# A graph-attention and message-passing kernel on one core: where in a half turn VectorE finishes a tile

## The chip, the cores and the metric

One Trainium2 chip, one of its cores. The metric is the device time of one execution in microseconds (us); the kernel before was run three times. The engines are PE (TensorE, matrix products), DVE (VectorE), ACT (ScalarE), POOL (GpSimd) and SP (SyncE, which only issues DMAs here). Each has its own instruction stream, executed in order, and they wait for each other through semaphores.

## What is computed

x is 8192 x 128, adj is an 8192 x 8192 matrix of zeros and ones, symmetric, with ones on the diagonal and about 0.4% of the rest. There are two layers, each with a layer norm before it and the residual added behind it:

```python
h = relu(layernorm(x))                       # layer 0: graph attention
Wh = h @ W;  f1 = Wh @ a1;  f2 = Wh @ a2
e = leaky_relu(f1 + f2.T, 0.2)
att = softmax(where(adj > 0, e, -9e15))
x = x + relu(att @ Wh)
h = relu(layernorm(x))                       # layer 1
node = h @ W1                                # 128 -> 16
m = einsum('nk,nkf->nf', node, einsum('nc,kcf->nkf', h, W2))
x = x + relu(adj @ m + node @ b)
```

## The kernel before, in words

**Blocks, turns, half turns.** The 8192 rows are 64 tiles of 128, in 8 blocks of 8 tiles. The attention loop (`attention_loop`, L297) goes through 8 blocks `ib`; a block is 4 turns `jg`, a turn two half turns `p`: 64 half turns in all, number n = 2i + p with i = 4 ib + jg. A half turn multiplies the 1024 rows of the block with 8 tiles of 128 neighbours. These 8 are called row tiles here; they come in four pairs k = 0 to 3, each with b = 0 and 1.

**What a half turn does for its own block.** adj comes in as float32, loaded by DMAs of the SP and ACT queues (`load_quadrants`, L325; SP loads quadrants 0 and 1 of each of four parts c, ACT 2 and 3). ACT casts each loaded part in two halves h to bytes (`cast`, L613, instruction L617), DVE transposes the bytes in squares of 32 (`turn_squares`, L1030) into the mask `mt`, four transposes (semaphore `squared`) a half turn, always for the next half turn. For each row tile DVE writes a 128 x 1024 weight tile p_sb with one instruction (`weigh`, L1109, instruction L1113). There are four buffers of p_sb, r = 2(k mod 2) + b, so a weigh of pair k waits (`p_used[r]`) until PE is done with the row tile of the same b in pair k-2; for k = 2 that is pair 0 of the same half turn. PE takes a row tile with 16 matmuls (L911). The mask is also stored to DRAM (`maskT_d`) by the ACT queue, for layer 1.

**What a half turn does for a tile of the block before.** From the second block on (56 half turns; `finish` is true) each half turn also finishes one tile m of the block before: it completes the attention output, normalises the row, and makes the message. The steps, by engine:
- DVE `finish_tile` (L1079). Step 0: `att` from the sums (L1084). Step 1: divide and relu (L1089), wait for `kept`, add x into `keep` (L1094), `bn_stats` (L1097), `bn_aggr` (L1100, semaphore `mv_done`). Step 2: wait for ACT's `std`, reciprocal (L1103), `xn` (L1106, `xn_done`). In `turn` (L1117) each step stands between the two weighs of a pair: step 0 in pair 0, step 1 in pair 1, step 2 in pair 2. After the second weigh of each pair comes one `turn_squares`.
- PE `finish_turn_h` (L885) waits for `xn_done` and transposes xn (L889). It stands in `half_turn` (L891) directly behind the first row tile of pair 2. After pair 2 PE multiplies by W1 and b (L877) and by the first half of W2 (L882, two groups), after pair 3 by the second half of W2 (L882).
- ACT `finish_tile` (L671): `std` at k = 1; at k = 2 first a cast, then relu of the transpose (L669), copies (L683, L685) and 8 scalings of PE's products by `node` (L693); 8 more at k = 3. Between `std` and the relu stand two casts.
- POOL `finish_tile` (L492): `confirm` (L477) waits until the stores of the tile before have landed and raises `kept`; then `fold` (L483) adds the 16 scaled products in three shrinking additions (L487) and a last one (L490), two instructions split the message (L502, L504), and two DMAs store `msg` and `keep`. `keep` and `msg` have two buffers each, so DVE's step 1 of tile m needs the stores of tile m-2.

```python
if finish and k < 3:
    finish_tile(k, p, u, 2 * u + p, 2 * jg + p, ib - 1)      # DVE, turn, L1129
if finish and k == 2 and b_ == 0:
    finish_turn_h(m)                                        # PE, half_turn, in front of the second row tile
```

**Setup** (the first 53 us). x is normalised, projected, and the bounds of the scores are found. DVE casts the lower halves of parts 0 to 2 of the first adj load (`first_cast`, L1037) and turns them; ACT casts part 3 and, after the exponentials (L645 to L653), the upper halves of parts 0 to 3. Between these it issues its share of the loads of the next turn (`load_upper`, L605), each part as soon as its upper half is cast; SP does so for its share. In the first turn DVE's transposes for the next turn stand one behind each pair of the second half turn.

**Layer 1.** `gather` (L946) runs four passes over the stored masks and messages, converted by DVE (L1160) and ACT (L716); during the first pass the last block's 8 tiles are finished (`finish_last`, another schedule). At the very end ACT stores the last 1024 rows (`store_out`, L762) in two groups of four DMAs, each when its rows are ready.

Of the kernel before, what the change touches and what calls it, by code (L numbers as in the profile page):

```python
# [29 lines left out]
ALU = mybir.AluOpType  # L30
# [8 lines left out]
def build(nc, x, adj, W, a1, a2, W1, W2, b, out):  # L39
# [34 lines left out]
    with ctx:  # L74
# [261 lines left out]
        def load_x_pair(eng, i, quadrants):  # L336
            for c in quadrants:
                eng.dma_start(rows_of_pair(i)[c * SQ:(c + 1) * SQ, :, :],
                              x_v[group(i, c):group(i, c) + 2].rearrange("h r t f -> r h (t f)")).then_inc(x_in[i], 16)

        def load_xt(eng, pb):
            eng.wait_ge(mv_done, T * pb + 1)
            for c in range(A):
                eng.dma_start(xt[c * SQ:(c + 1) * SQ, :, :], x_v[bass.ds(group(pb, c), 1)]
                              .rearrange("g r t f -> (g r) t f")).then_inc(xt_in, 16)


        @block.sync
        def _(sp):

            sp.sem_inc(xt_in, 16 * A)
            for i in range(1, 4):
                load_x(sp, i, (0, 1))
            for i in range(4, NB, 2):
                load_x_pair(sp, i, (0, 1))
            load_x(sp, 0, (0, 1))
            for c in range(A):
                load_quadrants(sp, 0, 0, c, (0, 1))

            def turn(i, ib, jg, rows=False):  # L360
                for c in range(A):
                    if isinstance(i, int) and i == 1:
                        sp.wait_ge(adj_cast[0][c], 1)
                    sp.wait_ge(adj_cast[1][c], i)
                    load_quadrants(sp, ib, jg, c, (0, 1))
                    if rows and c == 2:
                        load_xt(sp, ib - 1)

            def turns(ib, first, rows=False):
                for jg in range(first, IT):  # L370
                    turn(ib * IT + jg, ib, jg, rows and jg == 1)

            turns(0, 1)
            sp.dma_start(wcat[:, 0:K * D].rearrange("c (k f) -> c k f", f=D),
                         W2.rearrange("k c f -> c k f")).then_inc(w2_in, 16)
            turns(1, 0)
            with sp.Fori(0, NB - 2) as before:
                turns(before + 2, 0, True)

            for c in range(A):  # L380
                sp.wait_ge(adj_cast[1][c], NB * IT)
            for p in range(2):
                sp.wait_ge(mt_stored[p], 16 * 2 * IT)

            def load_messages(s):
                o = ORDER[s]
                sp.dma_start(msgs[:, o * T:(o + 1) * T, :, :].rearrange("p n c f -> p (n c f)").bitcast(FP32),
                             msg_d[:, o * T:(o + 1) * T, :].rearrange("p n f -> p (n f)").bitcast(FP32))\
                  .then_inc(msgs_in[s], 16)

            def load_masks(ii, s):
                q = s % 4

                if isinstance(ii, int) and s >= 4:
                    sp.wait_ge(conv_dve, dve_count(True, (s - 3) * T - 1, 1))
                    sp.wait_ge(conv_act, act_count(True, (s - 3) * T - 1, 1))
                elif not isinstance(ii, int):
                    sp.wait_ge(conv_dve, first_dve + (ii - 1) * NT + (s - 3) * T)
                    sp.sem_inc(past_sp, 1)
                    done = act_count(True, (s + 5) * T - 1, 1) if s < 4 else first_act + (s - 3) * T  # L400
                    sp.wait_ge(conv_act, (ii - 1) * NT + done)
                    sp.sem_inc(past_sp, 1)
                sp.dma_start(masks_w[:, q, :, :],
                             maskT_d[ORDER[s], bass.ds(2 * ii, 2), :, :].rearrange("i p w -> p i w"))\
                  .then_inc(masks_in[q], 16)

            def load_kept(ii):
                sp.wait_ge(out_ready, ii * 4 + 4)
                sp.dma_start(keeps[:, :, :], keep_d[:, bass.ds(2 * T * ii, 2 * T), :]).then_inc(keeps_in, 16)

            for s in range(4):
                load_masks(0, s)
            sp.wait_ge(squared, A * NB * NB)
            sp.wait_ge(kept, (ORDER[0] + 1) * T + 2)
            load_messages(0)
            for p in range(2):
                sp.wait_ge(mt_stored[p], 16 * NB * IT)
            for r in range(4):
                sp.wait_ge(p_used[r], 4 * NB * IT)
            for s in range(1, NB - 1):  # L420
                sp.wait_ge(kept, (ORDER[s] + 1) * T + 2)
                load_messages(s)
            for s in range(4, NB):
                load_masks(0, s)
            load_kept(0)
            with sp.Fori(0, NB // 2 - 1) as before:
                for s in range(NB):
                    load_masks(before + 1, s)
                sp.wait_ge(kept, NT + 2)
                load_kept(before + 1)  # L430


        @block.gpsimd
# [137 lines left out]
        def _(act):  # L571
# [41 lines left out]
            def cast(c, h, count, squared_before):  # L613

                act.wait_ge(adj_in[c], 16 * A * count)
                act.wait_ge(squared, squared_before)
                act.activation(m8[:, h, c, :].rearrange("p (t n) -> p t n", n=COLS), adj_halves[:, c, :, h, :],  # L617
                               ACT.Copy, scale=EDGE).then_inc(adj_cast[h][c], 1)
# [11 lines left out]
            for i in range(NB):  # L630
# [10 lines left out]
                if i == NB - 2:  # L641
                    act.activation(std[:, :], eps[:, :], ACT.Exp)
            cast(3, 0, 1, 0)
            act.wait_ge(setup_dve, 12)
            act.activation(bcol[:, :], fcol[:, :, 1], ACT.Exp, bias=shifts[:, 0:1]).then_inc(setup_act, 1)  # L645
            act.activation(qcol[:, :], fcol[:, :, 1], ACT.Exp, bias=shifts[:, 1:2], scale=SLOPE - 1.0)\
# [4 lines left out]
                   .then_inc(z0_copied, 1)  # L651
            act.wait_ge(zcol_done, 1)
            act.activation(zcol[:, :], zcol[:, :], ACT.Exp, scale=1.0 - SLOPE).then_inc(setup_act, 1)  # L653
            for c in range(A):
                cast(c, 1, 1, 0)
                if c < 3:
                    load_upper(1, c)
# [101 lines left out]
                act.activation(yT[:, 2 * ib * HB:(2 * ib + 1) * HB], acc_ps[2 * ib][:, :], ACT.Copy, scale=1.0 / EDGE)\  # L759
                   .then_inc(y_act, 1)  # L760

            def store_out(ii, h):  # L762
                act.wait_ge(out_ready, 4 * ii + 2 * h + 6)
                for c in range(A):
                    act.dma_start(out_v[bass.ds(ii * 2 * A + 2 * c + h, 1)].rearrange("g r t f -> (g r) t f"),
                                  outs[c * SQ:(c + 1) * SQ, h * T:(h + 1) * T, :]).then_inc(out_stored, 16)

            convert(0, True, 1)
            for t in range(NT):
# [24 lines left out]
            for h in range(2):  # L794
                take_bank(NB // 2 - 1, h)
            for h in range(2):
                store_out(NB // 2 - 1, h)
            act.wait_ge(out_stored, 16 * A * NB + 128)


# [192 lines left out]
        def _(dve):  # L993
# [40 lines left out]
                dve.wait_ge(adj_cast[0][c], 1)  # L1034
                turn_squares(0, c)

            def first_cast(c):  # L1037
                dve.wait_ge(adj_in[c], 16 * A)
                dve.tensor_scalar(m8[:, 0, c, :].rearrange("p (t n) -> p t n", n=COLS), adj_halves[:, c, :, 0, :],
                                  EDGE, None, ALU.mult).then_inc(adj_cast[0][c], 1)  # L1040

            for c in range(3):
                first_cast(c)
                first_squares(c)
            dve.wait_ge(wh_copied, 3 * NB)
            dve.sem_inc(setup_dve, 1)
            dve.tensor_reduce(ext[:, 0:1], fcol[:, :, 1], AX.X, ALU.max).then_inc(setup_dve, 1)
# [69 lines left out]
            def turn(i, ib, jg, finish, last):  # L1117
                for p in range(2):
                    n = 2 * i + p
                    u = i - IT  # L1120
                    for k in range(C):
                        tile = (2 * jg + p) * T + 2 * k
                        if k == 0:
                            dve.wait_ge(squared, A * n + A)

                        weighed = p == 0 and k < 2 and isinstance(jg, int) and jg == 0
                        if not weighed:
                            weigh(n, i, ib, p, k, 0, tile)
                        if finish and k < 3:  # L1129
                            finish_tile(k, p, u, 2 * u + p, 2 * jg + p, ib - 1)  # L1130
                        if not weighed:
                            weigh(n, i, ib, p, k, 1, tile)
                        if not finish and k == 1 and not (ends_block(jg) and p == 1):
                            scale_rows(n + 1)
                        if not (last and p == 1):
                            dve.wait_ge(adj_cast[1 - p][k], i + 1 + p)
                            if k == 0 and not (isinstance(i, int) and i == 0 and p == 0):
                                dve.sem_inc(past_dve, 1)
                                dve.wait_ge(mt_stored[1 - p], 16 * (i + p))
                            turn_squares(1 - p, k)  # L1140

            def start_weights(ib):

# [106 lines left out]
```

## Time and profile before

| | us |
|---|---|
| three runs | 1733.82 median (1728.38 to 1735.62) |
| the profiled execution | 1729.3 |
| its span, first to last instruction | 1727.5 |
| PE busy in the span | 1687.0 (98%) |
| DVE busy | 1310.1 (76%) |
| ACT busy | 1087.5 (63%) |
| POOL busy | 682.6 (40%) |
| mean granted clock of PE | 0.996 of full speed |

The stages in the span: setup to 53 us, first block of the attention loop (nothing to finish) to about 180 us, seven blocks that finish tiles to about 1207 us, the gather to 1716 us, the last rows to the end. Adding DMAs, the 16 DMA engines are busy nearly all of the attention loop. In the timelines an instruction that waits for the completion of another shows "[idle before <- who ended it]"; an instruction that has started but can't proceed shows as longer than its like.

### The profile page before, as it was taken

What the parts mean: (1) busy time and instruction counts of PE and PEld (TensorE: products, weight loads), DVE (VectorE), ACT (ScalarE), POOL (GpSimd) and SP (SyncE); (2) the same over time, 40 slices, a digit from 0 to 9 for tenths busy, and PEclk for the clock granted to TensorE, in tenths of its full rate; (3) what the DMA queues carried; (4) which work ended last, traced back from release to release, by engine and by line L of the source; (5) the groups of instructions that cost most, each with busy time, mean ns of one, the idle gap of its engine ahead of it and who ended that gap; (6) DMA issues with size and microseconds to landing.
All of it is one profiled execution on the core that took longest, in us unless ns stands there. A gap on an engine that the chain in (4) does not pass through costs nothing.

```text
span 1727.5 us, 34517 instructions
## 1 busy us (share of the span) xinstructions
PE 1687.0 (98%) x11268; PEld 1460.1 (85%) x11268; DVE 1310.1 (76%) x1748; ACT 1087.5 (63%) x1886; POOL 682.6 (40%) x560
## 2 busy tenths in 40 slices
PE   7899999999999999999999999999999999999997
PEld 5799988888888898898888988988677888888886
DVE  7788888989889889889898998887656543533434
ACT  5654666776766776766767767663565555556554
POOL 6000256556556565565564664654544100000000
PEclk9999999999999999999999999999999999999999
DMA  9899999999999999999999999967543345354430
GB/s 295 269 377 365 372 299 311 305 306 311 305 302 314 306 307 320 298 311 320 294 310 318 296 318 303 306 193 300 232 166 112 141 169 191 132 198 149 166 146 24
DMA packets 170704, 451.65 MB, mean 261 GB/s; under 512 B 13489, under 2 KB 13585, under 8 KB 152865
## 3 DMA queue, kind: packets, MB, share of 16 engines
q1 hardware_dynamic: 82304, 223.37, 41.1%
q10 hardware_dynamic: 81072, 206.10, 38.3%
q0 software_dynamic: 7280, 21.59, 3.7%
q8 instruction: 25, 0.41, 0.1%
q14 instruction: 23, 0.18, 0.0%
HBM read 363.94 MB, written 87.07 MB: 261 GB/s over the span
## 4 chain that ended last, share of the span: by engine, by line
PE 65%; DMA 12%; POOL 9%; DVE 5%; issue 5%; ACT 2%; ACTq 1%; POOLq 0%; DVEq 0%; SPq 0%
PE ot_ps L911 28%; PE mt_ps L970 13%; PE ot_ps L970 13%; PE hw_ps L882 9%; DMA keep_d<-keep 6%; POOL prod L487 5%; DMA maskT_d<-mt 3%; DVE p_sb L1113 3%; DMA adj_sb<-in_adj_dram 2%; POOL msg L490 1%; DVE mt L1031 1%; ACT prod L693 1%; POOL p_sb L459 1%; POOL msg L502 1%; PE h_ps L877 1%
## 5 line engine op out<-in xcount | busy, mean ns | idle before, releaser
L911 PEld LDWEIGHTS ot_ps<-wh_mask,p_sb 128*128 128x128 f32 x8192 | 942.5, 192 | 76.4 <-issue 70.3
L911 PE MATMUL ot_ps<-wh_mask,p_sb 128*128 (+1 forms) x8192 | 950.8, 276 | 17.2 <-DVE p_sb L1113 17.2
L1113 DVE SCALAR_TENSOR_TENSOR p_sb<-zb,qcol,mt 128x1024 f32<-128x1024 uint8 (+1 forms) x512 | 742.8, 1466 | 20.7 <-DVE mt L1031 9.9
L487 POOL TENSOR_TENSOR prod<-prod 128x1024 f32<-128x1024 f32 (+2 forms) x192 | 397.4, 2070 | 449.9 <-ACT prod L693 374.6
L617 ACT ACTIVATE wh_mask<-adj_sb 128x2048 uint8<-128x2048 f32 x253 | 481.6, 1935 | 59.6 <-DMA adj_sb<-in_adj_dram 44.5
L1160 DVE CAST mask<-adj_sb 128x1024 fp32r<-128x1024 uint8 x272 | 204.0, 757 | 244.6 <-PE mt_ps L970 242.6
L716 ACT ACTIVATE mask<-adj_sb 128x1024 fp32r<-128x1024 uint8 x240 | 255.2, 1064 | 173.7 <-PE ot_ps L970 173.5
L693 ACT ACTIVATE prod<-hw_ps,node 128x128 f32<-128x128 f32 x1024 | 278.7, 383 | 114.2 <-PE hw_ps L882 113.3
L970 PE MATMUL mt_ps<-mask,msgs 128*128 128x512 f32 x1024 | 282.5, 398 | 1.9 <-DVE mask L1160 1.0
L970 PE MATMUL ot_ps<-mask,msgs 128*128 128x512 f32 x1024 | 274.7, 390 | 0.8
L882 PE MATMUL hw_ps<-wcat,hT 128*128 128x512 f32 x512 | 240.7, 592 | 0.0
L970 PEld LDWEIGHTS mt_ps<-mask,msgs 128*128 128x128 f32 x1024 | 191.1, 188 | 51.0 <-issue 13.0
L970 PEld LDWEIGHTS ot_ps<-mask,msgs 128*128 128x128 f32 x1024 | 191.6, 188 | 43.6 <-issue 3.5
L1031 DVE STREAM_TRANSPOSE mt<-wh_mask 128x512 f32<-128x512 f32 x256 | 179.7, 702 | 23.3 <-ACT wh_mask L617 11.5
L882 PEld LDWEIGHTS hw_ps<-wcat,hT 128*128 128x128 f32 x512 | 88.6, 190 | 61.8 <-issue 61.2
L669 ACT ACTIVATE hT<-h_ps 128x128 f32<-128x128 f32 x64 | 17.8, 278 | 129.8 <-PE h_ps L889 129.5
L490 POOL TENSOR_TENSOR msg<-prod 128x128 f32<-128x128 f32 x64 | 87.9, 1373 | 5.0
L1094 DVE TENSOR_TENSOR keep<-att,xt 128x128 f32<-128x128 f32 x64 | 28.3, 442 | 79.0 <-POOLq L481 72.3
L683 ACT ACTIVATE node<-h_ps 128x16 f32<-128x16 f32 x64 | 11.8, 184 | 104.7 <-PE h_ps L877 104.7
L1106 DVE TENSOR_SCALAR xn<-keep,mv,rstd 128x128 f32<-128x128 f32 x64 | 59.9, 936 | 2.3
L515 POOL DMA_DIRECT2D zb<-zrow_d x7 | 3.8, 537 | 115.1 <-DVE p_sb L1113 96.0
L507 POOL DMA_DIRECT2D msg_d<-msg x56 | 31.7, 566 | 43.5 <-ACT keep L685 22.2
(129 smaller groups left out, 572.8 us busy)
## 6 DMA issues: line engine op xcount, KB each, us to landing
adj_sb<-in_adj_dram SPq DMA_DIRECT2D x256, 512.0 KB, 11.1
adj_sb<-in_adj_dram ACTq DMA_DIRECT2D x256, 512.0 KB, 12.2
adj_sb<-maskT_d SPq DMA_DIRECT2D x32, 2048.0 KB, 7.7
maskT_d<-mt ACTq DMA_DIRECT2D x62, 1024.0 KB, 10.2
keep_d<-keep POOLq DMA_DIRECT2D x64, 128.0 KB, 5.4
p_sb<-keep_d SPq DMA_DIRECT2D x4, 2048.0 KB, 11.8
msg_d<-msg POOLq DMA_DIRECT2D x56, 128.0 KB, 5.4
msgs<-msg_d SPq DMA_DIRECT2D x7, 1024.0 KB, 8.8
```

What stands on the lines that cost most here:

```text
L487: pool.tensor_tensor(prod[:, 0:n, :], prod[:, 0:n, :], prod[:, n:2 * n, :], ALU.add)\
L490: pool.tensor_tensor(msg32[:, :], prod[:, 0, :], prod[:, 1, :], ALU.add).then_inc(prod_read, 1)
L617: act.activation(m8[:, h, c, :].rearrange("p (t n) -> p t n", n=COLS), adj_halves[:, c, :, h, :], ACT.Copy, scale=EDGE).then_inc(adj_cast[ ...
L693: ins = act.activation(prod[:, head, :], hw_ps[g % 2][:, j * D:(j + 1) * D], ACT.Copy, scale=node[:, head:head + 1])
L716: act.activation(mask32[:, r, ib, :], masks[:, s % 4, ib, t % T // 4, :, t % 4], ACT.Copy)\
L882: pe.matmul(hw_ps[g % 2][:, :], hT[:, :], wcat[:, g * HB:(g + 1) * HB], start=True, stop=True)\
L911: ins = pe.matmul(ot_ps[h][:, (t - t0) * ROW:(t - t0 + 1) * ROW], p_sb[:, r, t * P:(t + 1) * P], rows, start=begin and t == t0, stop=end a ...
L970: ins = pe.matmul(acc_ps[2 * ib + h][:, :], msgs[:, ORDER[s] * T + t % T, c, :], mask32[:, r, ib, h * HB:(h + 1) * HB], start=t == 0 and c ...
L1031: dve.transpose(mt_squares[:, p, c, :, :, :], m8_squares[:, p, c, :, :, :]).then_inc(squared, 1)
L1106: dve.tensor_scalar(xn[:, :], x1, mv[:, 0:1], rstd[:, :], ALU.subtract, ALU.mult)\
L1113: dve.scalar_tensor_tensor(p_sb[:, r, :], zbf[:, bass.ds((ib % 2) * BLK, BLK)], qcol[:, bass.ds(tile + b_, 1)], mtb[:, p, k // 2, :, 2 * ( ...
L1160: dve.tensor_copy(mask32[:, r, ib, :], masks[:, s % 4, ib, t % T // 4, :, t % 4])\
```

## The change

It has four parts.

1. In every half turn that finishes a tile, DVE's step 1 (which writes `keep`) moves from pair 1 to pair 2, and step 2 (which writes xn) from pair 2 to pair 3. Step 0 stays. The streams of PE, ACT and POOL in the half turn are not touched.
2. In the setup, DVE casts the upper half of part 0 too, and ACT issues its share of the next load of part 0 ahead of its exponentials and casts only parts 1 to 3.
3. In the second half turn of the first turn, DVE's four transposes for the next turn stand behind all of its weighs, not one behind each pair.
4. The eight last stores are issued half by SP and half by ACT.

```diff
--- before.py
+++ after.py
@@ -338,6 +338,11 @@
                 eng.dma_start(rows_of_pair(i)[c * SQ:(c + 1) * SQ, :, :],
                               x_v[group(i, c):group(i, c) + 2].rearrange("h r t f -> r h (t f)")).then_inc(x_in[i], 16)
 
+        def store_rows(eng, ii, h, quadrants):
+            for c in quadrants:
+                eng.dma_start(out_v[bass.ds(ii * 2 * A + 2 * c + h, 1)].rearrange("g r t f -> (g r) t f"),
+                              outs[c * SQ:(c + 1) * SQ, h * T:(h + 1) * T, :]).then_inc(out_stored, 16)
+
         def load_xt(eng, pb):
             eng.wait_ge(mv_done, T * pb + 1)
             for c in range(A):
@@ -428,6 +433,9 @@
                     load_masks(before + 1, s)
                 sp.wait_ge(kept, NT + 2)
                 load_kept(before + 1)
+            for h in range(2):
+                sp.wait_ge(out_ready, 4 * (NB // 2 - 1) + 2 * h + 6)
+                store_rows(sp, NB // 2 - 1, h, (0, 1))
 
 
         @block.gpsimd
@@ -641,6 +649,7 @@
                 if i == NB - 2:
                     act.activation(std[:, :], eps[:, :], ACT.Exp)
             cast(3, 0, 1, 0)
+            load_upper(1, 0)
             act.wait_ge(setup_dve, 12)
             act.activation(bcol[:, :], fcol[:, :, 1], ACT.Exp, bias=shifts[:, 0:1]).then_inc(setup_act, 1)
             act.activation(qcol[:, :], fcol[:, :, 1], ACT.Exp, bias=shifts[:, 1:2], scale=SLOPE - 1.0)\
@@ -651,7 +660,7 @@
                    .then_inc(z0_copied, 1)
             act.wait_ge(zcol_done, 1)
             act.activation(zcol[:, :], zcol[:, :], ACT.Exp, scale=1.0 - SLOPE).then_inc(setup_act, 1)
-            for c in range(A):
+            for c in range(1, A):
                 cast(c, 1, 1, 0)
                 if c < 3:
                     load_upper(1, c)
@@ -759,11 +768,9 @@
                 act.activation(yT[:, 2 * ib * HB:(2 * ib + 1) * HB], acc_ps[2 * ib][:, :], ACT.Copy, scale=1.0 / EDGE)\
                    .then_inc(y_act, 1)
 
-            def store_out(ii, h):
+            def store_out(ii, h, quadrants=(0, 1, 2, 3)):
                 act.wait_ge(out_ready, 4 * ii + 2 * h + 6)
-                for c in range(A):
-                    act.dma_start(out_v[bass.ds(ii * 2 * A + 2 * c + h, 1)].rearrange("g r t f -> (g r) t f"),
-                                  outs[c * SQ:(c + 1) * SQ, h * T:(h + 1) * T, :]).then_inc(out_stored, 16)
+                store_rows(act, ii, h, quadrants)
 
             convert(0, True, 1)
             for t in range(NT):
@@ -794,7 +801,7 @@
             for h in range(2):
                 take_bank(NB // 2 - 1, h)
             for h in range(2):
-                store_out(NB // 2 - 1, h)
+                store_out(NB // 2 - 1, h, (2, 3))
             act.wait_ge(out_stored, 16 * A * NB + 128)
 
 
@@ -1034,14 +1041,15 @@
                 dve.wait_ge(adj_cast[0][c], 1)
                 turn_squares(0, c)
 
-            def first_cast(c):
+            def first_cast(c, h):
                 dve.wait_ge(adj_in[c], 16 * A)
-                dve.tensor_scalar(m8[:, 0, c, :].rearrange("p (t n) -> p t n", n=COLS), adj_halves[:, c, :, 0, :],
-                                  EDGE, None, ALU.mult).then_inc(adj_cast[0][c], 1)
+                dve.tensor_scalar(m8[:, h, c, :].rearrange("p (t n) -> p t n", n=COLS), adj_halves[:, c, :, h, :],
+                                  EDGE, None, ALU.mult).then_inc(adj_cast[h][c], 1)
 
             for c in range(3):
-                first_cast(c)
+                first_cast(c, 0)
                 first_squares(c)
+            first_cast(0, 1)
             dve.wait_ge(wh_copied, 3 * NB)
             dve.sem_inc(setup_dve, 1)
             dve.tensor_reduce(ext[:, 0:1], fcol[:, :, 1], AX.X, ALU.max).then_inc(setup_dve, 1)
@@ -1126,18 +1134,23 @@
                         weighed = p == 0 and k < 2 and isinstance(jg, int) and jg == 0
                         if not weighed:
                             weigh(n, i, ib, p, k, 0, tile)
-                        if finish and k < 3:
-                            finish_tile(k, p, u, 2 * u + p, 2 * jg + p, ib - 1)
+                        if finish and k != 1:
+                            finish_tile(k - k // 2, p, u, 2 * u + p, 2 * jg + p, ib - 1)
                         if not weighed:
                             weigh(n, i, ib, p, k, 1, tile)
                         if not finish and k == 1 and not (ends_block(jg) and p == 1):
                             scale_rows(n + 1)
-                        if not (last and p == 1):
+                        if not (last and p == 1) and not (isinstance(i, int) and i == 0 and p == 1):
                             dve.wait_ge(adj_cast[1 - p][k], i + 1 + p)
                             if k == 0 and not (isinstance(i, int) and i == 0 and p == 0):
                                 dve.sem_inc(past_dve, 1)
                                 dve.wait_ge(mt_stored[1 - p], 16 * (i + p))
                             turn_squares(1 - p, k)
+                    if isinstance(i, int) and i == 0 and p == 1:
+                        dve.wait_ge(mt_stored[0], 16)
+                        for c in range(A):
+                            dve.wait_ge(adj_cast[0][c], 2)
+                            turn_squares(0, c)
 
             def start_weights(ib):
```

## Rows read from the trace of the kernel before

**Rows 1.** Page, part 1: busy time of each engine.
```profile
PE 1687.0 (98%) x11268; PEld 1460.1 (85%) x11268; DVE 1310.1 (76%) x1748; ACT 1087.5 (63%) x1886; POOL 682.6 (40%) x560
```

**Rows 2.** Waits: engine line waited for: us in total, times, longest us.
```profile
ACT hT L669 <- PE h_ps L889: 129.5, 60, 7.5
...
DVE keep L1094 <- POOLq L481: 72.3, 46, 5.6
...
PE ot_ps L911 <- DVE p_sb L1113: 17.2, 30, 3.7
```

**Rows 3.** Timeline (start us, us, instruction), PE: first, a middle, and last transposes of 56.
```profile
189.86 0.27 PE L889 MATMUL h_ps<-ident,xn 128*128 128x128 f32 x1
...
1160.76 0.27 PE L889 MATMUL h_ps<-ident,xn 128*128 128x128 f32 x1
...
1169.90 9.10 PE L911 MATMUL ot_ps<-wh_mask,p_sb 128*128 x80
1178.84 0.27 PE L889 MATMUL h_ps<-ident,xn 128*128 128x128 f32 x1
...
1199.48 0.27 PE L889 MATMUL h_ps<-ident,xn 128*128 128x128 f32 x1
```

**Rows 4.** Timeline, DVE, the same half turn.
```profile
1167.80 0.28 DVE L1089 TENSOR_SCALAR att<-att,rden 128x128 f32<-128x128 f32 x1
...
1168.97 1.25 DVE L1113 SCALAR_TENSOR_TENSOR p_sb<-zb,qcol,mt 128x1024 f32<-128x1024 f32 x1
...
1171.89 3.12 DVE L1113 SCALAR_TENSOR_TENSOR p_sb<-zb,qcol,mt 128x1024 f32<-128x1024 f32 x1 [1.04 <-PE ot_ps L911]
1174.93 0.15 DVE L1103 RECIPROCAL rstd<-std 128x1 f32<-128x1 f32 x1
1175.12 1.11 DVE L1106 TENSOR_SCALAR xn<-keep,mv,rstd 128x128 f32<-128x128 f32 x1
1176.15 1.27 DVE L1113 SCALAR_TENSOR_TENSOR p_sb<-zb,qcol,mt 128x1024 f32<-128x1024 f32 x1
1177.34 0.70 DVE L1031 STREAM_TRANSPOSE mt<-wh_mask 128x512 f32<-128x512 f32 x1
```

**Rows 5.** Timeline, POOL, the same half turn: the three additions of one fold.
```profile
1171.58 2.35 POOL L487 TENSOR_TENSOR prod<-prod 128x1024 f32<-128x1024 f32 x1 [6.05 <-ACT prod L693]
...
1174.00 2.14 POOL L487 TENSOR_TENSOR prod<-prod 128x512 f32<-128x512 f32 x1
...
1176.22 1.79 POOL L487 TENSOR_TENSOR prod<-prod 128x256 f32<-128x256 f32 x1
```

**Rows 6.** Timeline, DVE, a stretch in which POOL adds nothing.
```profile
187.28 0.35 DVE L1106 TENSOR_SCALAR xn<-keep,mv,rstd 128x128 f32<-128x128 f32 x1
```

**Rows 7.** PE timeline at two pauses; windows (us, busy by engine, PEclk, DMA share, GB/s).
```profile
91.68 0.60 PE L911 MATMUL ot_ps<-wh_mask,p_sb 128*128 x3 [3.69 <-DVE p_sb L1113]
...
1195.38 2.05 PE L911 MATMUL ot_ps<-wh_mask,p_sb 128*128 128x129 f32 x16 [1.88 <-DVE p_sb L1113]
...
46.00:50.00 4.00, 3.49 (x15) 1.49 (x14) 3.24 (x14) 2.81 (x5) 0.65 (x1) 1.00 0.01 2
92.00:96.00 4.00, 4.00 (x25) 4.00 (x24) 4.00 (x5) 1.94 (x2) 0.00 (x0) 0.61 1.06 368
1193.00:1199.00 6.00, 3.97 (x33) 3.59 (x32) 5.96 (x5) 0.02 (x1) 5.76 (x4) 1.00 1.02 388
```

**Rows 8.** Timelines of the setup: DVE, then ACT with its queue.
```profile
46.43 0.27 DVE L1047 TENSOR_REDUCE ext<-wh_mask 128x1 f32<-128x64 f32 x1 [1.57 <-ACT wh_mask L602]
...
51.47 1.89 ACT L617 ACTIVATE wh_mask<-adj_sb 128x2048 uint8<-128x2048 f32 x1
53.44 1.49 ACTq L327 DMA_DIRECT2D adj_sb<-in_adj_dram  x2
55.04 1.91 ACT L617 ACTIVATE wh_mask<-adj_sb 128x2048 uint8<-128x2048 f32 x1 [1.68 <-issue]
```

**Rows 9.** Timeline, ACT queue, the last stores.
```profile
1720.98 4.41 ACTq L765 DMA_DIRECT2D out_dram<-zb  x8
```

## The prediction, made before the change was built or run

> **What bounds the kernel now.** I read the page first: PE is busy 98% of the span [rows 1], so only what makes PE pause or lets it pause less can move the time. The waits come next [rows 2]. The one that part 1 of the change aims at is large, 72.3 us in 46 waits of DVE's L1094 for the stores of POOL, but it is DVE's. PE itself waited only 17.2 us for weigh tiles in the whole run. So I looked at PE's timeline from one transpose of xn (L889) to the next, where one half turn is a closed cycle [rows 3]: 1160.76 to 1178.84 is 18.08 us, and PE pauses nowhere in it. From the first L889 at 189.86 to the 56th at 1199.48 are 55 such intervals and 1009.62 us, 18.36 each. At 18.08 they would be 994.4, so the finishing half turns hold only 15.2 us of pauses. That is the most that a perfect removal of the `kept` wait can bring.
>
> **Part 1, the moved steps.** PE's L889 stays behind the first row tile of pair 2 and waits for xn. PE can go no further without it. In the new order DVE writes xn behind the first weigh of pair 3. So in each half turn this chain must fit: PE frees the buffer of its first row tile, DVE weighs the first tile of pair 2 into it, then step 1, the second weigh of pair 2, a transpose, the first weigh of pair 3, step 2; then L889. The first link can't be got round by running ahead, for the buffer is the one that PE is reading.
>
> The times come from the half turn that ends at 1178.84. PE's 80 matmuls from 1169.90 to 1178.84 are 0.112 us each, so the first 16 are issued by 1171.69. DVE stood waiting for exactly this (1.04 us) and began its weigh at 1171.89 [rows 3, 4]. That weigh took 3.12 us, where its like take 1.25, because POOL's first addition had begun at 1171.58 and ran its 2.35 us to 1173.93 first [rows 4, 5]. This is no accident of one half turn: the fold starts when ACT has scaled PE's last products, and PE makes them right in front of that first row tile, so both clocks are set by PE. DVE is free at 1175.01. From there, in the new order:
> - POOL's second addition has stood waiting since 1174.00 and goes first. It ended at 1176.14 [rows 5]: 1.13 us. Today it holds up xn instead, which took 1.11 us there and 0.35 where POOL adds nothing [rows 4, 6].
> - Step 1 without a wait, from the start of L1089 to the start of the next weigh (1167.80 to 1168.97): 1.17. The `kept` wait itself goes, as step 1 comes one weigh, one transpose and one weigh later than now.
> - Weigh, start to start (1176.15 to 1177.34): 1.19. Transpose (0.70 from 1177.34, less the 0.08 by which neighbours overlap): 0.62. Weigh again: 1.19.
> - Reciprocal, start to start: 0.19, then xn 0.35 [rows 4, 6].
>
> The sum is 5.84, so xn is ready at 1180.85 and L889 can run at about 1180.95, where PE wanted it at 1178.84: a pause of 2.1 us in each half turn. POOL's third addition, 0.59 alone (it waited for a weigh until 1177.42 and ended at 1178.01), may also slip into the chain; I put in 0.2 for it. **Taken: 2.3 us.** Bounds: without any hold by the second and third additions 1.0; with the third in full, and a last small one of about 0.3 (an estimate, half of the third), 3.0.
>
> The pause feeds on nothing and recovers nothing: after L889 PE has two row tiles ready, and DVE, with 10.9 us from L889 to the freed buffer and about 8 us of work for it (five weighs of 1.19, three transposes of 0.62, step 0 of some 0.3), is back at the buffer's wait in time, again just behind POOL's start. So the half turn becomes 18.08 + 2.3 = 20.38 us, and 55 of them 1120.9: **+111.3 us** against 1009.6. This already takes in that the 15.2 us of old pauses go.
>
> What else hangs on it: ACT's `std` waits for step 1 in front of two casts of 1.89 [rows 8]. Step 1 ends about 1177.3, `std` and casts about 1181.4, the transposed xn is there at 1181.2, and ACT stood idle 2.2 us on average there [rows 2]; PE asks for the relu only 16 matmuls (1.8 us) later. Cost nothing; if this cover went, about 1 us a half turn. POOL's stores and DVE's transposes come later by the pause like everything else.
>
> [...] In the rows, xn beside an addition is slow as well, though it reads one tensor; I have therefore let the second addition hold up L1089, an instruction of the same form, in full. [...]
>
> **Part 2, the setup.** DVE idles 1.57 us in front of L1047; the new cast is at most what ACT takes for the same shape, 1.89 (an estimate), so it hangs over by 0.3 us at worst [rows 8]. ACT's casts and loads come 3.57 us apart (51.47 to 55.04), so parts 1 to 3 move up by that and part 0 by some 7 us, into a time when the DMA engines are idle (share 0.01) [rows 7, 8]. ACT's two early DMA issues (1.49) lie beside a cast. Then PE's pauses of the first block shrink, the last of which is 3.69 us before 91.68 [rows 7]. Bounds: 0 and -8 us. Taken: **-4**, about the 3.57.
>
> **Part 3.** The four transposes come later, but the last of them could not be earlier than its cast, and the weigh that PE waits for at 91.68 stands behind that last one in both. Their like cost 0.62 each; cost 0, between -1 and +2 (three transposes that were spread before).
>
> **Part 4.** Eight issues take 4.41 us in one queue [rows 9], 0.5 each; the last four are the end of the kernel, and two of them go to SP's idle queue: **-1**, between -1 and 0.
>
> **Sum.** 111.3 - 4 - 1 = +106 us. On the profiled execution (1729.3, span 1727.5) that is 1835; the median of the three runs is 4.5 higher, 1733.8, which gives **1840 us**.
>
> **The rivals.**
> - *Faster: the chain fits.* Without POOL in it, the chain is 1.19 + 5.84 - 1.13 = 5.90 us from 1171.89, xn is there at 1177.8, and PE never waits. The old pauses go: 1733.8 - 15 - 5 = **1714 us**. It decides if POOL's holds cost under 1.0 us a half turn in this place. For it: DVE's 72.3 us of waits go for certain, and it has slack then. Against: the first addition alone held DVE for 2.04 us, and it starts ahead of the freed buffer.
> - *A shorter pause.* Only the first addition counts, or DVE and POOL fall in a kinder order: 1.0 to 1.5 us, 19.1 to 19.6 a half turn, **1774 to 1802 us**.
> - *The clock falls too.* After a pause of 3.69 us the granted clock was 0.61 in the 4 us that followed; after one of 1.88 us it stayed 1.00 [rows 7]. The new pauses lie between. [...]
> - *Nothing to measure.* The pause and the gains cancel, or the order in the built streams isn't what the diff says: **1734 us**.
>
> **Chances.** Forecast mechanism at 1.5 to 3.0 us of pause: 0.70. Shorter pause: 0.11. Slow clock or more: 0.05. Faster: 0.09. Nothing: 0.05. 0.5% (9 us) is about what a measurement of this kernel can tell from no change. Slower by more: 0.86, within: 0.05, faster by more: 0.09. The range takes the first two cases, 1.0 to 3.0 us of pause: 55 x 19.08 is +40, 1774 us, and 55 x 21.08 is +150, less about 4, 1880 us.
>
> **What would show it.** In the new profile PE should wait for DVE's L1106 in front of L889 some 55 times, near 2.3 us each and over 100 us in total, a wait that is nearly absent now. L889 should come every 20.4 us. L1094's wait for POOL should be near 0, DVE's wait for PE in front of L1113 should have grown, and the weigh of pair 2 should still take about 3.1 us. The clock should stay 1.00. Wrong would be: intervals of 18.1 (the faster rival), or pauses that stand elsewhere, as ACT's `std` or relu. PE's pause in front of the third half turn should shrink by about 4 us, and the last store should be issued by both queues.

## The result and the profile after

The changed kernel takes 1886.92 us (median of 4 runs, 1882.91 to 1891.16) against 1734.02 before, **8.8% more**: the ratio is 1.0877, 95% interval 1.085 to 1.0903. I had forecast 1840 us and a range of 1774 to 1880. The direction was right. The size was not, and the measured time lies above the range. The profiled executions, from which all rows come, took 1888.5 and 1729.3 us, 159 us apart; the medians are 153 apart. One of the eight runs of the kernel with POOL's additions cut down took 1910.22 us at a mean granted clock of 0.848 and is left out of its figures below.

The page of the changed kernel (span; busy time and share), to be held against [rows 1]:

```profile
span 1886.5 us, 34516 instructions
...
PE 1722.6 (91%) x11268; PEld 1479.6 (78%) x11268; DVE 1364.5 (72%) x1749; ACT 1091.9 (58%) x1885; POOL 565.1 (30%) x560
```

PE's share fell from 98 to 91%. Its busy time rose by 36 us though it does the same work, a first sign that it ran at a lower clock for a while (mean granted clock 0.984, 0.996 before). The waits (engine line waited for: us in total, times, longest us; L896 is the transpose of xn, L1121 the weigh, L1102 the addition of x into keep, L684 std, L678 the relu), against [rows 2]:

```profile
ACT std L684 <- DVE mv L1108: 253.6, 57, 6.4
...
DVE p_sb L1121 <- PE ot_ps L918: 180.8, 159, 3.2
...
PE h_ps L896 <- DVE xn L1114: 135.1, 57, 2.5
...
ACT hT L678 <- PE h_ps L896: 16.9, 15, 3.7
...
PE ot_ps L918 <- DVE p_sb L1121: 5.3, 6, 1.5
...
DVE keep L1102 <- POOLq L489: 4.8, 1, 4.8
```

PE now waits 57 times for xn, 135.1 us in all, a wait that is nearly absent before. DVE's wait for POOL's stores, the target of part 1, fell from 72.3 to 4.8 us (one wait, behind the loop), and PE's waits for weighs from 17.2 to 5.3 (10.7 in the run of part 1 alone). DVE itself now waits 180.8 us for PE to free buffers. ACT has hardly any slack left in front of the relu (16.9 us in all, 129.5 before). PE's timeline, to be held against [rows 3]:

```profile
887.37 0.32 PE L896 MATMUL h_ps<-ident,xn 128*128 128x128 f32 x1 [2.48 <-DVE xn L1114]
...
896.73 9.10 PE L918 MATMUL ot_ps<-wh_mask,p_sb 128*128 x80
908.25 0.32 PE L896 MATMUL h_ps<-ident,xn 128*128 128x128 f32 x1 [2.42 <-DVE xn L1114]
...
929.18 0.33 PE L896 MATMUL h_ps<-ident,xn 128*128 128x128 f32 x1 [2.48 <-DVE xn L1114]
...
951.73 0.33 PE L896 MATMUL h_ps<-ident,xn 128*128 128x128 f32 x1 [2.42 <-DVE xn L1114]
```

From 887.37 to 908.25 is 20.88 us, and PE has run dry for 2.4 us of it. The next but one interval, 929.18 to 951.73, is 22.55 us. The whole loop from the first to the 56th transpose takes 1169.5 us (185.00 to 1354.45), against 1009.6. Of the 55 intervals 42 lie between 20.4 and 21.0 us, and 13 between 22.4 and 22.6. Nothing is added to the 13 but this, here for the one that begins at 929.18 (windows: us, PE busy, PEld busy, DVE, ACT, POOL, granted clock, DMA share, GB/s):

```profile
925.00:929.00 4.00, 1.71 (x16) 1.51 (x14) 3.81 (x8) 3.50 (x3) 2.90 (x5) 1.00 1.02 387
929.00:933.00 4.00, 3.82 (x20) 3.43 (x21) 3.74 (x6) 1.04 (x4) 0.01 (x1) 0.71 1.06 243
933.00:937.00 4.00, 4.00 (x23) 2.79 (x22) 1.41 (x2) 2.73 (x9) 0.00 (x0) 0.87 1.00 249
```

PE runs dry at the end of the window that begins at 925. Behind the pause the granted clock is 0.71 over one 4 us window and 0.87 over the next, which is about 1.7 us of full speed lost: the difference between 20.9 and 22.55. In windows of 1 us it is 0.50 from 931 to 934. There are 13 such falls of the clock in the loop, one for each long interval; before the change the loop has none.

DVE's chain in the half turn that ends with the transpose at 929.18, to be held against [rows 4]:

```profile
919.71 3.02 DVE L1121 SCALAR_TENSOR_TENSOR p_sb<-zb,qcol,mt 128x1024 f32<-128x1024 uint8 x1 [1.60 <-PE ot_ps L918]
922.65 1.28 DVE L1097 TENSOR_SCALAR att<-att,rden 128x128 f32<-128x128 f32 x1
924.07 0.73 DVE L1102 TENSOR_TENSOR keep<-att,xt 128x128 f32<-128x128 f32 x1
924.84 0.29 DVE L1105 BATCH_NORM_STATS2 stat<-keep 128x6 f32<-128x128 f32 x1
925.29 0.18 DVE L1108 BATCH_NORM_AGGREGATE mv<-stat 128x2 f32<-128x6 f32 x1 [0.16 <-DVE stat L1105]
925.43 1.30 DVE L1121 SCALAR_TENSOR_TENSOR p_sb<-zb,qcol,mt 128x1024 f32<-128x1024 uint8 x1
926.65 0.70 DVE L1038 STREAM_TRANSPOSE mt<-wh_mask 128x512 f32<-128x512 f32 x1
927.28 1.24 DVE L1121 SCALAR_TENSOR_TENSOR p_sb<-zb,qcol,mt 128x1024 f32<-128x1024 uint8 x1
928.44 0.15 DVE L1111 RECIPROCAL rstd<-std 128x1 f32<-128x1 f32 x1
928.63 0.41 DVE L1114 TENSOR_SCALAR xn<-keep,mv,rstd 128x128 f32<-128x128 f32 x1
```

and POOL beside it, against [rows 5] (first line: the three additions in one; last line: the third alone):

```profile
919.29 5.36 POOL L495 TENSOR_TENSOR prod<-prod 128x1024 f32<-128x1024 f32 x3 [11.21 <-ACT prod L702]
924.73 0.46 POOL L498 TENSOR_TENSOR msg<-prod 128x128 f32<-128x128 f32 x1
...
923.93 0.73 POOL L495 TENSOR_TENSOR prod<-prod 128x256 f32<-128x256 f32 x1
```

DVE waits 1.60 us for the buffer, just as foreseen, gets it at 919.71 behind POOL's first addition (919.29), and its weigh takes 3.02. L1097, the division, took 1.28 instead of 0.28: POOL's second addition held it. (The forecast had let the second addition hold this instruction in full, and L1097 took 1.28 or 1.29 in 55 of 56 half turns.) L1102 took 0.73 instead of 0.29: POOL's third addition (923.93 to 924.66) held that one as well. xn itself is short now, 0.41.

### The profile page after: what moved, and what is told of

It is laid out like the page before. It is cut to its first block, busy times and chain, and to the rows that moved or that the text cites. A ratio compares the mean times of both kernels' runs of the same rounds, so it can differ in the third digit from the quotient of the medians.

```text
span 1886.5 us, 34516 instructions
## 1 busy us (share of the span) xinstructions
PE 1722.6 (91%) x11268; PEld 1479.6 (78%) x11268; DVE 1364.5 (72%) x1749; ACT 1091.9 (58%) x1885; POOL 565.1 (30%) x560
## 4 chain that ended last, share of the span: by engine, by line
PE 60%; DVE 16%; issue 13%; DMA 7%; POOL 1%; ACT 1%; DVEq 1%; ACTq 1%; SPq 0%; POOLq 0%
PE ot_ps L918 22%; PE mt_ps L977 12%; PE ot_ps L977 12%; PE hw_ps L889 11%; DVE p_sb L1121 5%; DVE att L1097 4%; DMA maskT_d<-mt 3%; DVE mt L1038 2%; DVE keep L1102 2%; DMA adj_sb<-in_adj_dram 2%; DMA xt<-in_x_dram 1%; DVE xn L1114 1%; PE h_ps L896 1%; PE h_ps L884 1%; DVE stat L1105 1%
## 5 line engine op out<-in xcount | busy, mean ns | idle before, releaser
L1121 DVE SCALAR_TENSOR_TENSOR p_sb<-zb,qcol,mt 128x1024 f32<-128x1024 uint8 (+1 forms) x512 | 749.5, 1471 | 193.5 <-PE ot_ps L918 180.8
L495 POOL TENSOR_TENSOR prod<-prod 128x1024 f32<-128x1024 f32 (+2 forms) x192 | 333.8, 1739 | 732.0 <-ACT prod L702 717.3
L889 PE MATMUL hw_ps<-wcat,hT 128*128 128x512 f32 x512 | 250.6, 613 | 0.0
L684 ACT ACTIVATE std<-mv,eps 128x1 f32<-128x1 f32 x64 | 19.3, 302 | 253.6 <-DVE mv L1108 253.6
L896 PE MATMUL h_ps<-ident,xn 128*128 128x128 f32 x64 | 20.4, 319 | 135.1 <-DVE xn L1114 135.1
L896 PEld LDWEIGHTS h_ps<-ident,xn 128*128 128x128 f32 x64 | 8.9, 139 | 146.3 <-issue 140.5
L512 POOL TENSOR_TENSOR msg<-msg 128x128 fp32r<-128x128 f32 x56 | 72.7, 1298 | 4.5
L1097 DVE TENSOR_SCALAR att<-att,rden 128x128 f32<-128x128 f32 x64 | 73.3, 1145 | 0.3
L1102 DVE TENSOR_TENSOR keep<-att,xt 128x128 f32<-128x128 f32 x64 | 43.9, 685 | 15.0 <-POOLq L489 4.8
```

The lines of the kernel that those rows point to most:

```text
L495: pool.tensor_tensor(prod[:, 0:n, :], prod[:, 0:n, :], prod[:, n:2 * n, :], ALU.add)\
L889: pe.matmul(hw_ps[g % 2][:, :], hT[:, :], wcat[:, g * HB:(g + 1) * HB], start=True, stop=True)\
L1097: dve.tensor_scalar(att[:, :], att[:, :], rden[:, bass.ds(t, 1)], 0.0, ALU.mult, ALU.max)\
L1102: dve.tensor_tensor(x1, att[:, :], xt[:, bass.ds(t, 1), :].rearrange("p t f -> p (t f)"), ALU.add)\
L1121: dve.scalar_tensor_tensor(p_sb[:, r, :], zbf[:, bass.ds((ib % 2) * BLK, BLK)], qcol[:, bass.ds(tile + b_, 1)], mtb[:, p, k // 2, :, 2 * ( ...
```

## The experiments

Ten kernels. Time is the median, and a ratio is to the kernel before in runs on the same chip, with its 95% interval. Intervals between transposes of xn are medians over the 55, from the profiled execution. The theory: part 1 alone costs the time, since PE's transpose waits for a chain of DVE work that begins at a buffer which PE frees in the same half turn, and POOL's additions make it too long to fit; the pauses then cost the clock. The rivals: other parts carry some of the loss; the chain is too long without POOL; the falls of the clock have another cause.

**Part 1 alone.** The DVE lines of part 1, on the kernel before.

```diff
-if finish and k < 3:
-    finish_tile(k, ...)
+if finish and k != 1:
+    finish_tile(k - k // 2, ...)
```

> Part 1 alone, on the kernel before. Chain theory (the whole slowdown is in part 1, since PE's transpose of xn waits for a chain that begins at a buffer PE frees in the same half turn): transposes of xn 20.9 us apart as in the changed kernel, and the other parts' gain of 5 us lost, so about 1892 us (1885 to 1898). Rival (the other parts, the setup or the deferred transposes, carry some of the loss, by shifting the DMAs against the attention loop): clearly under 1887 us.

Measured: 1891.16 us, ratio 1.0908 (1.0867 to 1.0949). Intervals of 20.92 us, 13 of them over 22.3. Its wait list:

```profile
PE h_ps L889 <- DVE xn L1106: 134.6, 57, 2.5
```

The whole loss is here: the ratio is as high as that of the changed kernel.

**Parts 2 to 4 alone.** The changed kernel with the lines above put back.

> Parts 2 to 4 without part 1. Chain theory: the attention loop is as before (18.1 to 18.5 us from one transpose to the next), the setup gives about 5 us and the tail 1, so 1728 us (1725 to 1731). Rival as above: 1740 us or more.

Measured: 1726.04 us, ratio 0.9961 (0.9945 to 0.9977). The loop takes 1009.4 us as before, and its first transpose comes at 186.16 instead of 189.86, 3.7 us earlier. These parts do no harm.

**POOL's additions cut down.**

```diff
-pool.tensor_tensor(prod[:, 0:n, :], prod[:, 0:n, :], prod[:, n:2 * n, :], ALU.add)
+pool.tensor_tensor(prod[:, 0:1, 0:8], prod[:, 0:1, 0:8], prod[:, n:n + 1, 0:8], ALU.add)
```

> The changed kernel, with POOL's three fold additions cut to 8 elements each (the messages are not summed, the rest is computed). If POOL's hold on DVE is what makes the chain too long: the chain falls from 9.4 us to about 6 us, below the 7 us that PE leaves for it, the transposes come 18.1 us apart, PE waits almost nowhere for xn, the clock stays up, and the time is 1710 to 1725 us. If the chain alone is too long (POOL has little part in it): the pause stays above 1.5 us and the time above 1800 us.

Measured: 1731.90 us, ratio 0.9989 (0.9967 to 1.001). DVE and, below it, PE of the same half turn:

```profile
516.95 0.28 DVE L1097 TENSOR_SCALAR att<-att,rden 128x128 f32<-128x128 f32 x1
517.38 0.40 DVE L1102 TENSOR_TENSOR keep<-att,xt 128x128 f32<-128x128 f32 x1
...
521.60 0.34 DVE L1114 TENSOR_SCALAR xn<-keep,mv,rstd 128x128 f32<-128x128 f32 x1
...
330.26 0.29 DVE L1102 TENSOR_TENSOR keep<-att,xt 128x128 f32<-128x128 f32 x1 [3.54 <-DMA xt<-in_x_dram]
```

```profile
504.50 0.27 PE L896 MATMUL h_ps<-ident,xn 128*128 128x128 f32 x1
...
513.65 9.10 PE L918 MATMUL ot_ps<-wh_mask,p_sb 128*128 x80
522.58 0.27 PE L896 MATMUL h_ps<-ident,xn 128*128 128x128 f32 x1
```

The order of the change is untouched, and PE runs from 504.50 to 522.58 in 18.08 us without a pause: 43 of the 55 intervals are 18.1 or 18.2 us. L1097 takes 0.28 again, and xn is there 0.6 us before PE asks for it. So the order alone fits, and POOL's additions are what makes it not fit. The time missed the expected 1710 to 1725, for a reason that I had not seen. The other 12 intervals, most of them in pairs at the start of a block, are long because the first tile of a block waits for its rows of x (the last line of the first fence: 3.54 us for the DMA) and PE's clock falls behind that pause in five cases of six (granted clock 0.72 over 6 us; in the sixth, behind 3.45 us, 1.00). In the changed kernel DVE waits for these rows only once, for 0.4 us.

**The pause filled.** Ten idle matmuls in front of the transpose; they write a PSUM bank that nobody reads then.

```diff
 if finish and k == 2 and b_ == 0:
+    idle_run(10, mt_ps[0])
     finish_turn_h(m)
```

> The changed kernel, with 10 idle bf16 matmuls of 512 columns (about 2.1 us) of PE in front of each transpose of xn, in the pause of about 2.6 us. If the pauses make the granted clock fall (13 intervals of 22.5 us among those of 20.9): the clock stays 1.00, all intervals are 20.9 us, and the time is about 21 us less, 1862 to 1868 us. If the falls come from something else: they stay, and the time is 1885 us or, where the filling costs, more.

Measured: 1864.19 us, ratio 1.0751 (1.0712 to 1.0789), 23 us less than the changed kernel. Wait and mean clock (0.984 in the changed kernel):

```profile
PE h_ps L896 <- DVE xn L1115: 15.5, 55, 0.4
```

```profile
core 0: 1862.1 us, clock 0.997
```

All 55 intervals are 20.4 to 20.9 us. The chain is as long as in the changed kernel, PE is just not idle while it waits, and no fall of the clock is left in the loop, which takes 1147.4 us instead of 1169.5. So the falls came from the pauses and cost about 22 us.

**Four idle matmuls**, the same edit with 4 in place of 10.

> The changed kernel with 4 idle matmuls (0.85 us) in front of each transpose of xn, so that a pause of about 1.7 us is left of 2.6. Intervals stay 20.9 us. If only pauses beyond about 2 us cost the clock: no falls, 1862 to 1868 us as with ten. If any regular pause does: some falls remain, 1870 to 1887 us. The runs with pauses of 1.0 to 1.2 us had none.

Measured: 1863.23 us, ratio 1.0763 (1.0745 to 1.0781), no fall in the loop.

```profile
PE h_ps L896 <- DVE xn L1115: 86.1, 56, 1.7
```

A pause of 1.5 to 1.7 us in every half turn did not cost the clock in this kernel; one of 2.4 to 2.5 us did, in 13 half turns of 55.

**xn one transpose and one weigh earlier.**

```diff
+if finish and k in (0, 2):
+    finish_tile(k // 2, ...)
 weigh(n, i, ib, p, k, 1, tile)
+if finish and k == 2:
+    finish_tile(2, ...)
```

> The changed kernel, but step 2 (xn) stands directly behind the second weigh of pair 2: one transpose and one weigh (1.8 us) leave the chain, nothing else moves. Chain theory: the pause falls from 2.8 to about 1.0 us, intervals near 19.1 us, the clock does not fall after so short a pause, 1760 to 1775 us. If POOL's instructions refill the room (a held DVE simply waits elsewhere in the chain), the interval stays over 19.8 us and the time over 1800 us.

Measured: 1782.22 us, ratio 1.0288 (1.0267 to 1.0308). Intervals of 19.35 us, no fall of the clock in the loop.

```profile
PE h_ps L896 <- DVE xn L1114: 37.0, 56, 1.2
```

1.8 us of work left the chain, and the interval fell by 1.6. The chain theory holds. The time lies above the expected 1760 to 1775; the interval was 0.25 us longer than the 19.1 expected, which is 14 us over 55. Most of that is a new wait of PE (its weight load for L884) for the relu, 12.7 us in all, because ACT's two casts behind std now end behind the transpose.

**Only xn moved.**

```diff
+if finish and k != 2:
+    finish_tile(min(k, 2), ...)
```

> The changed kernel, but step 1 stays in pair 1; only step 2 is in pair 3. Chain theory: step 1 (1.2 us) leaves the chain, intervals of 19.5 to 19.9 us, the wait of PE for xn 75 to 100 us in total, and fewer falls of the clock: 1800 to 1830 us. If step 1 in the chain was the whole trouble: under 1760 us.

Measured: 1783.84 us, ratio 1.0297 (1.0279 to 1.0315). Intervals of 19.09 us.

```profile
PE h_ps L896 <- DVE xn L1114: 45.0, 57, 1.9
...
DVE keep L1102 <- POOLq L489: 28.7, 20, 4.7
```

A miss: I had expected 19.5 to 19.9 and over 1800 us. Taking step 1 out of the chain saved 1.8 us, not 1.2. Its instructions are short and stand between POOL's, so POOL's third addition came in there. Without step 1 the second addition is followed by a weigh at once, and the third runs beside the transpose behind that weigh, which takes its usual 0.70 us:

```profile
916.76 1.60 POOL L495 TENSOR_TENSOR prod<-prod 128x256 f32<-128x256 f32 x1
...
917.69 0.70 DVE L1038 STREAM_TRANSPOSE mt<-wh_mask 128x512 f32<-128x512 f32 x1
918.32 1.24 DVE L1121 SCALAR_TENSOR_TENSOR p_sb<-zb,qcol,mt 128x1024 f32<-128x1024 uint8 x1
```

**The third addition cut down** (4 of 128 columns of it; the other two whole).

> The changed kernel, with only POOL's third fold addition cut (4 of 128 columns; the messages are partly not summed). The chain theory says that POOL's third addition stands in full between L1097 and L1102 of the chain (0.73 us from its start to its end in the trace of the changed kernel, and the forecast had put in 0.2): intervals fall from 20.9 to about 20.4 us, about 25 to 30 us less in all, 1855 to 1862 us, with the clock still falling. If DVE waits there for something else: 20.9 us and 1887 us.

Measured: 1840.61 us, ratio 1.0631 (1.061 to 1.0653).

```profile
959.93 1.28 DVE L1097 TENSOR_SCALAR att<-att,rden 128x128 f32<-128x128 f32 x1
961.25 0.31 DVE L1102 TENSOR_TENSOR keep<-att,xt 128x128 f32<-128x128 f32 x1
961.59 0.29 DVE L1105 BATCH_NORM_STATS2 stat<-keep 128x6 f32<-128x128 f32 x1
```

L1102 takes 0.31 instead of 0.73, the intervals are 20.41 instead of 20.93 us: the third addition stood in the chain with 0.52 us. That part came out as expected; the time missed the expected 1855 to 1862, because the clock falls in only 3 intervals instead of 13, behind pauses 0.5 us shorter (about 2.0 us). Of the 46 us between the two profiled executions some 25 to 29 are the shorter intervals and 17 the ten falls; the rest lies behind the loop (see the last stretch, below).

**Step 1 behind the second weigh of pair 1, xn in pair 2 as before.**

```diff
-if finish and k != 1:
-    finish_tile(k - k // 2, ...)
+if finish and k in (0, 2):
+    finish_tile(k, ...)
 weigh(n, i, ib, p, k, 1, tile)
+if finish and k == 1:
+    finish_tile(1, ...)
```

> The changed kernel, but step 1 stands behind the second weigh of pair 1 (one weigh later than in the kernel before) and step 2 in pair 2 as before. The chain from the freed buffer to xn is then as short as before. Chain theory: no pause at xn, the wait for kept falls by up to 1.2 us a half turn, and of the 15 us of pauses before a part goes: 1715 to 1726 us. If the wait for kept was no cause of PE's pauses: 1728 us, like parts 2 to 4 alone.

Measured: 1719.52 us, ratio 0.9928 (0.9912 to 0.9943).

```profile
ACT hT L678 <- PE h_ps L896: 114.5, 61, 7.5
...
DVE keep L1102 <- POOLq L489: 32.9, 38, 3.8
...
PE ot_ps L918 <- DVE p_sb L1121: 8.9, 9, 3.8
```

The wait for the stores fell from 72.6 us (parts 2 to 4 alone) to 32.9, and 51 of 55 intervals are 18.1 us against 37: the loop takes 997.3 us instead of 1009.4, and the profiled spans are 1712.1 and 1723.3. The profiled execution is the fastest of this kernel's six, though; by the medians the gain on parts 2 to 4 alone is about 6 us, not 11. This version beats both kernels: 0.7% under the kernel before and 9% under the changed one.

**Step 1 at the head of pair 2, xn in pair 2.**

```diff
+if finish and k == 2:
+    finish_tile(1, ...)
 if not weighed:
     weigh(n, i, ib, p, k, 0, tile)
```

> As the run before it, but step 1 stands at the head of pair 2, behind the transpose of pair 1 and in front of the first weigh of pair 2: 1.8 us later than in the kernel before. The wait for kept should be nearly gone, and the chain from the freed buffer does not hold step 1: 1713 to 1724 us. A rival: step 1 now meets POOL's first addition where it stands directly in front of the first weigh of pair 2, and delays that weigh: 1730 us or more.

Measured: 1722.51 us, ratio 0.9934 (0.9916 to 0.9951), not to be told apart from the run before it. 47 intervals of 18.1 us. The step's delay past one more transpose took only a little more of the wait (26.1 us), and PE waited 15.7 us for weighs, against 8.9.

## Why the forecast failed in size

**What bounds the kernel, and the chain: right.** The two ends of the chain, DVE's wait for the freed buffer, the first addition ahead of the weigh (3.02 us; forecast 3.12) and the second ahead of L1097 stand in the trace as written. PE's old pauses went, as forecast; whether the moved wait removed them, or only the slack that every longer half turn now has, these runs don't tell apart.

**Which step failed.** The clock is the step that failed: the forecast put it at nothing, and it cost 22 us. The range allowed for half turns of up to 21.08 us, which covers the measured 20.93, but held no fall of the clock; the two kernels with the pauses filled have the whole chain and no fall, and take 1864 and 1863 us, inside the range. The other part of the miss is mis-sized terms of the half turn: 20.93 us at the median against a forecast 20.38 (20.865 at the mean of those without a fall, 27 us in 55).

**The third addition: a mis-sized term.** "I put in 0.2 for it"; the run without it moved the interval by 0.52 us, nearly its full length alone (0.59). The step that failed is the treatment as a chance: POOL's third addition waits at the moment when L1097 ends, so it goes ahead of L1102 in every half turn. In the forecast's own rows it stood ready at 1176.22, and that was enough to place it. This is 0.3 of the 0.55 us.

**PE's side of the cycle: a term put at nothing.** After a wait for xn, PE takes 9.37 us (median) from the transpose to its last 80 matmuls, before 9.15; 0.11 of that is the first matmul behind the transpose, which comes after 0.22 us and not 0.11. From the first of the 80 to the weigh it is 2.10 us, in the forecast's row 1.99. With 0.04 more from xn to the transpose these are 0.37 us; the other terms of the chain were 0.1 us too long in the forecast.

**The clock: given 1 chance in 20, and it came.** I had a row of a 1.88 us pause without a fall and one of 3.69 us with a fall. I took the former as the nearer, although the forecast pause of 2.3 us lay beyond it, and although it was a single pause and the new ones come in every half turn. A fall like the one of [rows 7] (0.39 of 4 us lost, 1.6 us) in every half turn would have cost 88 us, an estimate; 13 of 55 had one, at 1.7 us each: 22 us. Pauses of 2.4 to 2.5 us brought the fall in 13 of 55 half turns, those of 1.5 to 1.7 us in none.

**Part 2.** Forecast -4; the runs with it have the first transpose 1.3 to 4.9 us earlier than the kernel before, 3.7 in the run of parts 2 to 4 alone, 4.9 in the changed kernel. Single executions differ by some 2 us here: part 1 alone, with the setup of before, has it at 191.85, the kernel before at 189.86. PE's pause in front of the third half turn, which was to shrink by about 4 us from 3.69, is 0.8 us in the changed kernel, but 2.1 to 4.1 in the other nine runs with part 2. **Part 3** shows no price apart from it. **Part 4** forecast -1. The stores are issued by two queues:

```profile
1880.23 3.44 SPq L343 DMA_DIRECT2D out_dram<-zb  x4
1880.24 3.51 ACTq L343 DMA_DIRECT2D out_dram<-zb  x4
```

The last group of rows is ready at 1882.86 and the kernel ends 3.7 us later, before it was 3.9: about 0.2 us gained.

**The last stretch: 4 us of this one execution.** From the 56th transpose to the end the changed kernel takes 532.1 us, the one before 528.0. DVE's second tile in the gather waits for stores of the last tile of the loop, and here PE waits in turn:

```profile
1379.14 0.29 DVE L1102 TENSOR_TENSOR keep<-att,xt 128x128 f32<-128x128 f32 x1 [4.75 <-POOLq L489]
...
1382.33 2.05 PE L977 MATMUL mt_ps<-mask,msgs 128*128 128x512 f32 x4 [3.04 <-DVE mask L1173]
```

The clock falls once more beside this pause (0.50 from 1382 to 1388). It is no cost of part 1: DVE waits at this place in the kernel before too (3.47 us, and PE then 0.73), and the run of part 1 alone and the two with filled pauses, which all have part 1, take 528.1 to 528.2 us from the 56th transpose to the end. Why the stores landed 1.2 us later in this execution is open.

**The sum, remade**, for the profiled executions. Before the first transpose -4.9. In the loop 55 x (20.865 - 18.08) = 153.2 without the clock (20.865 us is the mean of the 42 intervals without a fall), less 15.2 of old pauses, and 21.9 of clock: 159.9. Behind it +4.1. Together +159.1 us, and the spans differ by 159.0. Two small slips of the forecast change nothing in it: the first addition held the weigh for 1.87 us (3.12 less 1.25), not 2.04, and the lower end of the range leaves out the gains of parts 2 and 4, which the upper end counts.

## What to carry to other kernels

When work is moved to avoid a wait, first write down the closed cycle between the engines that it moves into, from a buffer's release to the instruction that the other engine can't pass, with the work of a third engine that can hold it; here a cycle that came out 2.8 us too long in each of 55 half turns cost 160 us with its falls of the clock, though the move took 68 us of waits off an engine that wasn't the bottleneck. The same step moved by one instruction only, outside that cycle, gained about 6 us by the medians. And where two engines' instructions take turns, as DVE's and POOL's did here, place one that stands waiting in the sum, don't average it: here POOL's third addition went in at the first gap (L1102 took 0.73 us, with that addition cut down 0.31).

## What the runs showed of the hardware

- DVE and POOL instructions took turns. In the loop of the changed kernel the weigh ran behind POOL's first addition, the second addition behind the weigh, L1097 behind that, the third addition behind L1097, L1102 behind that, and with nearly the same times in nearly all half turns: the weigh 3.0 to 3.15 us in 50 of 56 (2.8 to 2.9 in five), L1097 1.3 in 55, L1102 0.7 to 0.85 in 53. The time for which an instruction is held stands in its duration (the weigh 3.02 us instead of 1.25), not as idle time before it. The transpose took its 0.70 us beside an addition (917.69 in the run with only xn moved). I had not expected such a fixed order.
- A pause of PE of 2.4 to 2.5 us in every half turn brought the granted clock down to 0.50 of full speed for some 3.4 us in 13 of 55 half turns, every fourth or fifth, at 1.7 us each. Pauses of about 2.0 us (third addition cut down) did so in 3 of 55, and two of 2.5 and 2.6 us in the same run did not; those of 1.5 to 1.7 us (four idle matmuls ahead of them) and those of 0.5 to 1.7 us (xn moved; once 1.9) never did in the loop. Of six single pauses of 2.8 to 3.45 us (additions cut down) five brought a fall. Ten or four idle bf16 matmuls into a bank that is free were worth 23 us, with no other change.
